# An attention loop on one core: five units a block, instead of four, take half of their exponentials on VectorE

## What is computed

```python
q, k = (rotary(q, N), rotary(k, N))
ql, kl = (q @ U, k @ U)
att = jnp.einsum('bhnr,bhmr->bhnm', ql, kl) / math.sqrt(dk)
y = jax.nn.softmax(att, axis=-1) @ v
```

## Time and profile before

| | |
|---|---|
| Time, median of 3 runs | 2568.58 us (2567.5 to 2569.24) |
| The profiled execution | 2567.2 us, of which span 2565.4 us |
| Granted TensorE clock, mean | 0.992 |
| Busy share of the span | PE 97%, ACT 78%, DVE 69%, PEld 42% |
| Late units | 98, in blocks 6 to 30 |

### The profile page before, as it was taken

How to read it: one execution, slowest core, us unless ns; L and a number is a source line. 1 busy time by engine, 2 the same in 40 slices (tenths; PEclk the granted TensorE clock), 3 DMA queues, 4 the chain that set the end, 5 groups by cost and what they waited for, 6 DMA issues and landing times.

```text
span 2565.4 us, 41339 instructions
## 1 busy us (share of the span) xinstructions
PE 2498.2 (97%) x15898; PEld 1089.3 (42%) x15898; DVE 1773.7 (69%) x2520; ACT 2000.7 (78%) x2215; POOL 56.0 (2%) x105
## 2 busy tenths in 40 slices
PE   3999999999999999999999999999999999999998
PEld 2222222222222222222222222222258888888886
DVE  7377774578777787887878877788645565646563
ACT  2899999999999999999999999999952322322222
POOL 1010000200000000000000000000100000000000
PEclk8999999999999999999999999999999999999999
DMA  3566654933333323433333433334620101111000
GB/s 105 125 149 155 148 144 94 179 63 77 71 62 70 71 59 66 75 65 71 61 71 59 76 73 61 71 70 75 128 44 1 26 2 23 25 25 23 2 8 18
DMA packets 100959, 178.69 MB, mean 70 GB/s; under 512 B 31432, under 2 KB 57064, under 8 KB 100782
## 3 DMA queue, kind: packets, MB, share of 16 engines
q1 hardware_dynamic: 88718, 150.92, 29.0%
q0 software_dynamic: 10336, 23.53, 4.3%
q10 hardware_dynamic: 1728, 1.87, 0.3%
HBM read 150.73 MB, written 25.49 MB: 69 GB/s over the span
## 4 chain that ended last, share of the span: by engine, by line
PE 89%; ACT 5%; issue 4%; DVE 2%; DMA 1%; ACTq 0%; SPq 0%; DVEq 0%
PE PS L759 35%; PE PS L729 25%; PE PS L1290 18%; PE PS L1275 5%; ACT PB L819 3%; PE PS L1302 2%; PE PS L744 2%; ACT EXP L819 1%; PE PS L480 1%; PE PS L476 1%; PE PS L485 0%; PE PS L470 0%; PE PS L1253 0%; DMA KSL<-KSD 0%; PE PS L1261 0%
## 5 line engine op out<-in xcount | busy, mean ns | idle before, releaser
L819 ACT ACTIVATE PB<-PS 128x1024 f32<-128x1024 f32 x1852 | 1729.6, 1115 | 28.9 <-PE PS L729 24.0
L759 PE MATMUL PS<-PB,V 128*17 128x512 f32 x7408 | 976.5, 599 | 2.2 <-DVE accS L1038 1.3
L729 PE MATMUL PS<-QSL,KSL 49*128 49x512 f32 x3900 | 823.5, 465 | 13.7 <-DMA KSL<-KSD 6.8
L729 PEld LDWEIGHTS PS<-QSL,KSL 49*128 49x128 f32 x3900 | 347.0, 184 | 909.2 <-ACT PB L819 823.7
L841 DVE SCALAR_TENSOR_TENSOR EXP<-EXP 128x1024 f32<-128x1024 f32 x294 | 360.1, 1225 | 10.1
L1369 ACT ACTIVATE hfr<-PS,s 128x512 f32<-128x512 f32 x128 | 86.9, 689 | 300.6 <-PE PS L1290 300.5
L829 DVE TENSOR_SCALAR EXP<-PS 128x512 f32<-128x512 f32 x196 | 135.4, 691 | 184.7 <-PE PS L744 182.2
L759 PEld LDWEIGHTS PS<-PB,V 128*17 128x17 f32 x7408 | 122.8, 95 | 289.0 <-issue 216.8
L1290 PE MATMUL PS<-hidden_ar,wh1r 128*128 128x512 f32 x1024 | 237.7, 391 | 0.0
L1290 PE MATMUL PS<-hidden_br,wh2r 128*128 128x512 f32 x1024 | 235.3, 390 | 0.0
L1290 PEld LDWEIGHTS PS<-hidden_br,wh2r 128*128 128x128 f32 x1024 | 191.7, 188 | 39.5
(11 more groups left out here) (183 smaller groups left out, 1487.2 us busy)
## 6 DMA issues: line engine op xcount, KB each, us to landing
KSL<-KSD SPq DMA_DIRECT2D x255, 256.0 KB
KSL<-KSD SPq DMA_DIRECT2D x255, 128.0 KB
QSD<-qhl SPq DMA_DIRECT2D x32, 256.0 KB
QSL<-QSD SPq DMA_DIRECT2D x62, 132.0 KB
KSD<-khl SPq DMA_DIRECT2D x58, 128.0 KB
first_y<-in_mlp POOLq DMA_DIRECT2D x22, 256.0 KB, 5.3
first_x<-in_mlp POOLq DMA_DIRECT2D x22, 256.0 KB, 6.1
xg<-in_x SPq DMA_DIRECT2D x8, 512.0 KB, 7.9
```

What stands on the lines that cost most here:

```text
L729: ins = pe.matmul(PS[:, 2 * (pair % SLOTS) + e, :], KSL[r, q % 2, s, k * P:(k + 1) * P], QSL[r, b % 2, s, :], start=True, stop=True, tile_ ...
L759: ins = pe.matmul(ACC[i * VW:i * VW + DK + 1, :], V17[:, HT * h + u, c, :], probs[:, (i % 2) * QW:(i % 2 + 1) * QW], start=kt == 0, stop=k ...
L819: act.activation(probs, PS[:, slot:slot + 2, :].rearrange("p a b -> p (a b)"), ACT.Exp).then_inc(at["probs_ready"], 1)
```

## The change

Four things change. (1) `LATE_AT` has five late units a block, 7, 13, 19, 23 and 31, where it had 1, 11, 14 and 25; block 6 has three where it had two, so that there are 123 late units for 98. (2) The sums of a late unit stand in its own iteration (for unit 23 in that of unit 24), where they stood 5 to 12 units after it. (3) The polynomial is written as a product of two quadratic factors: five instructions of the SCALAR_TENSOR_TENSOR and TENSOR_TENSOR kind of 1024 columns for six, and three instructions of a turn follow the one ahead without a wait, where one did. The read of a head becomes `late_head_dve`. (4) VectorE reads head 0 of the next late unit in the middle of the present one's polynomial, so that `ey` has two buffers. Beside this, `late_scores_pe` waits for the block's queries, since unit 7's heads are scored in units 29 and 31 of the block before, and `block_dve` waits for the sums of all late units, since unit 31 is one.

```diff
@@ -80,11 +80,13 @@
-LATE_AT = {1: ((0, 1), (2, 1), (11, 3)), 11: ((5, 1), (9, 1), (19, 1)), 14: ((12, 3), (17, 1), (26, 0)),
-           25: ((22, 1), (24, 0), (30, 3))}
+
+
+LATE_AT = {7: ((-3, 1), (-1, 1), (7, 3)), 13: ((3, 1), (6, 0), (13, 3)), 19: ((11, 0), (12, 0), (19, 3)),
+           23: ((15, 0), (18, 0), (24, 3)), 31: ((21, 0), (23, 2), (31, 3))}
 LATE_BLOCKS = range(6, NB_ALL - 1)
-LATE = [KT * _b + _u for _b in LATE_BLOCKS for _u in LATE_AT if _b > 6 or _u > 11]
+LATE = [KT * _b + _u for _b in LATE_BLOCKS for _u in LATE_AT if _b > 6 or _u > 13]
 LATE_NUMBER = {_u: _k for _k, _u in enumerate(LATE)}
 PLACES = {}
 for _b in LATE_BLOCKS:
@@ -113,8 +115,8 @@
 ROOT_BITS = 1597463007.0
-POW2 = (1.0000001192092896, -0.6931469440460205, 0.24022120237350464, -0.05550713092088699, 0.009675541892647743,
-        -0.001327647129073739)
+POW2 = (-1.2068495750427246, 28.587703704833984, 353.92730712890625, 0.006471000611782074, -0.0013276472454890609,
+        -1.2902637720108032)
 LOG2E = 1.4426950408889634
 TO_WHOLE = ROUND + 127.0
@@ -194,9 +196,9 @@
         mlp = {}
         with ExitStack() as life:
-            _, EXP = scope(("below_EXP", [P, (2 * DC + HC) * HID], F32), ("EXP", [P, 7, 2 * QW], F32))
+            _, EXP = scope(("below_EXP", [P, (2 * DC + HC) * HID], F32), ("EXP", [P, 8, 2 * QW], F32))
             late_act, late_dve = [EXP[:, k, :] for k in (0, 1)], [EXP[:, k, :] for k in (2, 3)]
-            ey, et, ee = [EXP[:, k, :] for k in (4, 5, 6)]
+            ey, et, ee = [EXP[:, k, :] for k in (4, 5)], EXP[:, 6, :], EXP[:, 7, :]
             weights = weight_tiles(life, True)
             PB, KSL, QSL, V17, accS, Y, LS, rl, first_y, first_x = scope(
@@ -736,6 +738,7 @@
             b = unit // KT
             q, k = divmod(unit, KQ)
             pe.wait_ge(at["k_in"][q % 2], keys_in(at, 0, q))
+            pe.wait_ge(at["q_in"][b % 2], (b // 2 + b % 2) * 64)
             if n == 0 and e == 0:
                 pe.wait_ge(setup_read, len(USE))
             else:
@@ -819,30 +822,38 @@
                 act.activation(probs, PS[:, slot:slot + 2, :].rearrange("p a b -> p (a b)"),
                                ACT.Exp).then_inc(at["probs_ready"], 1)
+        def late_head_dve(v, k, e):
+
+            v.wait_ge(poly_scores, 2 * k + e + 1)
+            v.tensor_scalar(ey[k % 2][:, e * QW:(e + 1) * QW], MISC, LOG2E, -126.0, ALU.mult, ALU.max).then_inc(poly_read, 1)
+
         def exponentials_dve(v, s, unit):
             k = LATE_NUMBER[unit]
+            y = ey[k % 2]
             if k == 0:
                 setup_left(v)
-            for e in range(2):
-                v.wait_ge(poly_scores, 2 * k + e + 1)
-                v.tensor_scalar(ey[:, e * QW:(e + 1) * QW], MISC, LOG2E, -126.0, ALU.mult, ALU.max).then_inc(poly_read, 1)
+                late_head_dve(v, 0, 0)
+            late_head_dve(v, k, 1)
             v.wait_ge(poly_read, 2 * k + 2)
-            s.did(v.tensor_scalar(et, ey, 127.0, TO_WHOLE, ALU.min, ALU.add))
-            s.settle()
-            s.did(v.scalar_tensor_tensor(ee, et, TO_WHOLE, ey, ALU.subtract, ALU.subtract))
-            s.settle()
-            s.did(v.tensor_scalar(ey, ee, POW2[5], POW2[4], ALU.mult, ALU.add))
+            s.did(v.tensor_scalar(et, y, 127.0, TO_WHOLE, ALU.min, ALU.add))
+            s.settle()
+            s.did(v.scalar_tensor_tensor(ee, et, TO_WHOLE, y, ALU.subtract, ALU.subtract))
+            s.settle()
+            s.did(v.scalar_tensor_tensor(y, ee, POW2[0], ee, ALU.add, ALU.mult))
             s.did(v.tensor_scalar(et.bitcast(I32), et.bitcast(I32), 23, None, ALU.logical_shift_left))
             s.settle()
-            s.did(v.tensor_tensor(ey, ey, ee, ALU.mult))
-            s.settle()
-            for c in (3, 2, 1):
-                s.did(v.scalar_tensor_tensor(ey, ey, POW2[c], ee, ALU.add, ALU.mult))
-                s.settle()
+            s.did(v.tensor_scalar(ee, ee, POW2[4], POW2[3], ALU.mult, ALU.add))
+            s.did(v.scalar_tensor_tensor(y, y, POW2[1], y, ALU.add, ALU.mult))
+            s.settle()
+            if k + 1 < len(LATE):
+
+                late_head_dve(v, k + 1, 0)
+            s.did(v.scalar_tensor_tensor(y, y, POW2[2], ee, ALU.add, ALU.mult))
+            s.settle()
             if k >= 2:
                 v.wait_ge(late_free, k - 1)
-            v.scalar_tensor_tensor(late_dve[k % 2], ey, POW2[0], et, ALU.add, ALU.mult).then_inc(poly_ready, 1)
+            v.scalar_tensor_tensor(late_dve[k % 2], y, POW2[5], et, ALU.add, ALU.mult).then_inc(poly_ready, 1)
             v.wait_ge(poly_ready, k + 1)
         def check_dve(v, s, n):
@@ -1033,6 +1044,9 @@
             sums = accS[:, :].rearrange("p (b f) -> p b f", f=VW)
             s = Steps(v, at["dve_step"], 2 * b)
             v.wait_ge(at["probs_free"], IN_RING[KT * b + KT])
+            late = len([u for u in LATE if u < KT * b + KT])
+            if late:
+                v.wait_ge(late_free, late)
             if b > 0:
                 v.wait_ge(at["y_ready"], b)
             v.transpose(accS[:, :], ACC).then_inc(at["acc_saved"], 1)
```

## The result

The changed kernel takes 2544.2 us in the median of 4 runs (2542.8 to 2545.08), beside 2568.47 (2567.5 to 2569.24) for the kernel before: a ratio of 0.9911, with a 95% interval from 0.9899 to 0.9922. The forecast was 2544. The profiled execution went from 2567.2 to 2545.08 us, its span from 2565.4 to 2543.3.

A forecast was written before the change was run, and what follows sets the result against it. ScalarE was taken as the bound, 60 pairs at 0.917 us plus 0.6 of stalls a block. One pair fewer in 25 blocks gives 22.9 us, stalls 1.5: 2567.2 to 2542.8, with 1.4 for the median 2544; range 2539 to 2559.

The forecast's parts named there:

- The sum: Profiled execution 2567.2 - 22.9 (one ScalarE pair fewer in 25 blocks) - 1.5 (stalls) = 2542.8; median 1.4 above: 2544.
- smaller stalls: ScalarE's stalls go from 0.61 to 0.55 us a block, 25 x 0.06 = 1.5 us gained.
- VectorE's turn: One late unit's VectorE work, with the next head 0 read in its middle: 9.6 us.
- the two waits for a head 0: VectorE waits about 1.4 us for unit 19's head 0 and about 2.2 for unit 7's.
- the five margins: VectorE's polynomials end ahead of TensorE's late sums by 1.4, 0.5, 1.0, 0.3 and 0.4 us.
- the rival of a long turn: VectorE's turn exceeds 9.6 + 0.15 us, each microsecond costing 2 us a block; at 10.6, 2586 us; chance 0.08.
- The third rival: VectorE's successors without a wait start no earlier: turn 0.36 us longer, 14 us gained, 2554.6 us; chance 0.05.
- The stalls: ScalarE's stalls left: about 0.34 us behind unit 24, 0.1 at the block's end, 0.1 added: 0.55 a block.
- At no cost: Added waits for queries and in `block_dve`, and unit 13's keys, cost nothing; blocks 0 to 5 and the MLP untouched.
- The room falls from 1.8 to 0.7 us a block, so ScalarE stays the bound: TensorE's block was put at 53.4 us against ScalarE's new 54.1, if ScalarE's stalls stay small.
- the stations: Times in a block when TensorE reaches the late sums: 12.4, 22.5, 32.6, 41.4 and 53.3 us behind the transpose.
- The first rival: TensorE takes part of the gain: stalls 1.1 us, a block 55.2, 10 us gained, 2558 us; chance 0.12.

The follow-up runs named there:

- Four late units: The changed kernel with unit 19 ordinary again, so late units 7, 13, 23 and 31 a block: 2566.17 us, ratio 0.9991.
- the polynomial alone: The kernel before, old order with four late units, with only the polynomial in its new form: 2566.81 us, ratio 0.9994.
- the longer turn: The changed kernel with one more VectorE instruction of 256 columns in every turn, 0.32 us longer: 2560.77 us, ratio 0.9975.
- the old polynomial: The changed kernel, five late units, with the polynomial of degree 5 in its old form: 2653.8 us, ratio 1.0333.
- the doubled scores: The changed kernel with head 0 of each late unit scored twice, five small matmuls more a block: 2564.99 us, ratio 0.9993.
- the shifted head: The changed kernel with unit 7's head 1 scored in iteration 0, not in unit 31 of the block before: 2539.18 us, ratio 0.9893.
- unit 25: The changed kernel with unit 25 late in place of 23, its sums in its own iteration: 2682.56 us, ratio 1.0438.

## Why the prediction was right, and where it wasn't

**The sum held, with some luck in the last 2 us.** One pair fewer in each of 25 blocks and little else: 24.3 us measured between the medians of the first comparison, 24.4 in the sum. The trace has less: 22.1 us in the 24 blocks and 0.5 in block 6, 22.6. The forecast's 1.5 us from smaller stalls did not come, since they are 0.61 us a block, as before. That the medians differ by 24.3 all the same lies within the scatter of the runs: the profiled execution was the slowest of its four (2545.08 for a median of 2544.2), while that of the kernel before was below its median (2567.2 for 2568.47). Four late units and the polynomial alone show that nothing else gives anything, as forecast.

**VectorE's turn held**: 9.55 us for 9.6, built from rows that the old turn already had. The polynomials ended 10.9, 22.2, 31.8, 41.3 and 53.0 us behind the transpose (forecast 11.0, 22.0, 31.6, 41.1, 52.9), TensorE's late sums started at 12.6, 22.7, 32.8, 41.4 and 53.4 (forecast 12.4, 22.5, 32.6, 41.4, 53.3), and the two waits for a head 0 were 1.78 and 2.13 for 1.4 and 2.2. Of the five margins only that of unit 24 was wrong in sign: 0.3 forecast, and 0.06 late in fact. It had been the thinnest, and the rival of a long turn rested on it; the longer turn showed that rival's slope of 2, and the old polynomial a steeper one, 2.7. The third rival falls by the row at 1211.52.

**The stalls were near in sum**, 0.61 for 0.55: 0.29 behind unit 24 for 0.34, but 0.32 at the block's edge for 0.1. With a head scored in TensorE's wait at the edge the second is 0.08, so the forecast's 0.1 would have been right for that order. "At no cost" failed there too, if only by 0.1: the transpose follows the last sums 0.12 later than before.

**"The room falls from 1.8 to 0.7 us a block, so ScalarE stays the bound" was wrong**, and that is the mis-sized term. TensorE's block was put at 53.4. From the rows after it is 27 ordinary units at 1.65 (1247.30 to 1248.95), 5 late ones at 0.43 + 0.98, 10 late heads at some 0.22, and the wait of 0.42 at the edge: 44.6 + 7.0 + 2.2 + 0.4 = 54.2, not below ScalarE's 54.1. Two errors made most of it. A late unit's single pair was costed as half of a double, 0.33, though the earlier trace rows had one that took 0.43 (1267.80 to 1268.23), and the forecast even used it for the stations: 5 x 0.1. And the wait of the first sums for the transpose was not in the floor: 0.4. The kernel before hid it behind a late head, and the forecast did not ask what the new places would do to it.

Why the number came out all the same: TensorE's part was just as large as ScalarE's, so it cost what had been put down as stalls and left the sum alone. That was luck: a few tenths more on TensorE and the block would have grown by most of it, as the doubled scores show (0.88 for 1.1). The first rival's mechanism, that TensorE takes part, is there, though its 55.2 us a block are not.

Two things stay open: what makes the 0.5 us between TensorE's own 54.2 and the 54.69, and what a block without the double sums would take. Seen from ScalarE's 54.1, the difference is 0.32 at the edge, of which the shifted head took 0.24, and 0.29 behind unit 24.

## What to carry to other kernels

Where two engines each need nearly all of a period, a cut on one of them can give nothing, and an addition costs most of its time: here 0.88 of 1.1 us on TensorE, and 0.85 (54.69 to 55.54) for the one pair more on ScalarE with four late units. It matters where in the period a cut stands: 1 us off TensorE in a stretch that ScalarE holds gave 0.01, 0.22 moved into TensorE's wait at the edge gave all of it. So before "B has room" enters a sum, add up B's period from starts, with each kind of turn at its own row and with the waits that the loop's edge forces on it. And look for such a wait first when placing new work: here one line of the table put 0.22 us of matmul into 0.42 of waiting.

## What the hardware showed that was not expected

- TensorE's granted clock fell to its lower level (0.50, 1.2 GHz) after a wait of 2 us within an otherwise full loop, and was below 1.00 in the next three stretches of 2 us (0.90, 0.50, 0.74). After the same wait in another block of the same run it did not fall. The runs with the old polynomial and with unit 25 had a mean clock of 0.980 and 0.961 for 0.991, and blocks of 58.5 to 60.8 and of 58.9 to 64.8 us.
- A late head's matmul of 49x512 costs 0.22 where it follows others directly (1244.22 to 1244.44 in the changed kernel). A single pair ahead of sums costs 0.43 (1217.07 to 1217.50) and two pairs 0.66 (1247.30 to 1247.96): the first pair of a sequence is dearer than the second, 0.43 for 0.23.
